# Expert work one scan step later, and the first gate inputs copied inside SBUF, in a fused mixture-of-experts and GRU kernel

## The chip, the cores and the metric

The kernel runs on one core of a Trainium2 chip. Its time is the device time of one execution in microseconds (us), the median of several runs. A profile of one further execution shows every instruction of the engines: TensorE (PE, with its weight loads as PEld), VectorE (DVE), ScalarE (ACT), GpSimd (POOL) and SyncE's DMA queue (SP).

## The reference

The input x is 8 sequences of 512 positions with 256 features. Two stages follow each other.

```
# stage 0: mixture of experts, added to x
shared = silu(x @ w1) * (x @ w3) @ w2
s      = sigmoid(concat(x, cond) @ router_W)         # 8 experts, the best 2 of s + bias
routed = sum_e combine[e] * (gelu(x @ W1e[e]) @ W2e[e])
x = x + (shared + routed) / 3
# stage 1: a GRU over the 512 positions, added to x; H starts as cond
Z = sigmoid(x_t @ Wxz.T + bxz + H @ Whz.T + bhz)
R = sigmoid(x_t @ Wxr.T + bxr + H @ Whr.T + bhr)
C = tanh(x_t @ Wxh.T + bxh + (R * H) @ Whh.T + bhh)
H = Z * H + (1 - Z) * C
out_t = x_t + H @ Whq.T + bhq
```

Everything is float32. The scan has 512 dependent steps. The expert work of a position must be done before its scan step, but it depends on no H.

## The kernel before

**Tiles and pairs.** A tile is 16 positions of the 8 sequences, 128 rows; there are 32 tiles (NT) of 16 scan steps (TS). Expert work goes by pairs of tiles (NPAIR is 16). For a pair it is 144 "up" products (12 units of 12: 4 units of the shared expert, then 8 experts), each 128 x 128 weights by 256 columns, with the operands split into a high and a low part; then for each tile 9 groups of "down" products; then a transpose of the finished tile (x1T), four "projection" products that give the 768 gate inputs in two pieces q of 384 columns with two parts k each (`project`), and, after the tile's scan, two output products of 256 columns (`output`).

**One scan step.** TensorE makes the r product (r_bank, L1247) and the z product (zc_bank) from H (hist). ScalarE makes t_r and t_z, VectorE transposes t_r (t_rT) and makes rhT, TensorE makes the c product (zc_bank<-whT,rhT), ScalarE t_h, VectorE the new H (terms, then a scan instruction into hist). ScalarE also copies ("seeds") the next step's gate inputs into r_bank and zc_bank, from xs.

**Where the expert work stands.** The scan's engines run one written-out order. Each step has a place r from 0 to 31 in a span of two tiles, and a pair number p. `place_of` gives both from the tile n and step s; FIRST_STEP (L274) shifts the whole expert schedule against the scan. `fill_up` puts work between the z and the c product, `fill_rest` behind the c product. Tables say what stands in which place:

- UP_GAP2: five up products in most places, behind the c product; UP_FIRST for pair 1, with five or six in a place. Up products of pair 1 with numbers under FIRST_UPS (36) and the down products of places under FIRST_R run ahead of the scan.
- DOWNS1: down products between z and c. A place takes three halves of 128 columns.
- PROJ1 (L279): the four projection products of a tile, in places 2 to 5 and 18 to 21, between z and c. OUT2: the two output products in place 2 or 18, behind c.
- BIAS2: VectorE's `add_bias` for a finished piece of gate inputs, at the end of a step; FINISH2: `finish_out`, which adds the output product and x; LATE_XT2: the transposes of later input tiles.
- UP_ACT2_FIRST, SILU1_FIRST and HIDDEN1_FIRST: where ScalarE and VectorE take pair 1's finished up products (`consume_up`, `shared_silu`, `shared_hidden`); an up product of a later unit waits for them, since there are two buffers.

**The gate inputs' way.** `add_bias` writes xproj in SBUF. SyncE's queue stores it to DRAM (`store_inputs`, L474), one DMA for each piece, and when the store has landed reads it back into xs (`gate_rows`, L480) with another layout, row = sequence, column = step: four DMAs, one for each of four column groups j, for steps 0 to 7 (semaphore xs_first) and four for steps 8 to 15 (xs_second). For the first tile this stands ahead of the scan. ScalarE waits for xs_first before its first seed. The queue issues in program order and a wait in it holds everything behind it; the loads of later tiles (L464) and the stores of the output stand in the same queue.

## Time and profile before

| what | value |
|---|---|
| median of 3 runs | 1277.98 us (1277.16 to 1278.83) |
| the profiled execution | 1277.44 us, span 1275.5 us |
| PE busy | 1249.8 us, 98% of the span |
| DVE busy | 997.2 us, 78% |
| ACT busy | 803.3 us, 63% |
| DMA | 51.34 MB, mean 40 GB/s |

The span is from the first to the last instruction; the profiled execution's own time has 1.94 us more around it. The ends of matmuls are modelled, so a high busy share of PE is not a proof that TensorE sets the time. The idle time of an engine counts where it stands on the path that ends last.

### The profile page before, as it was taken

Reading aid. Unit: us, or ns where it says so; the run is one execution under the profiler, and the core shown is the slowest. Engines: PE = TensorE matmul, PEld = TensorE weight load, DVE = VectorE, ACT = ScalarE, POOL = GpSimd, SP = SyncE. Lnnn points to the kernel's source line nnn. Section 1 sums busy time; section 2 is a strip of 40 time slices with the busy share of each in tenths; the row PEclk is TensorE's granted clock in tenths of the full one; section 3 lists DMA queues with packets and bytes.
Section 4 is the critical chain, followed back from the end, with each engine's and each line's share of the span. In section 5 each row is a group of like instructions: output and inputs, shape, how many; then the busy total and the mean of one; then the engine's idle time right before and its main releaser. Section 6 shows DMA issues by size and latency. Waiting matters only on the chain.

```text
span 1275.5 us, 84499 instructions
## 1 busy us (share of the span) xinstructions
PE 1249.8 (98%) x35704; PEld 890.8 (70%) x35704; DVE 997.2 (78%) x6111; ACT 803.3 (63%) x4402; POOL 7.4 (1%) x25
## 2 busy tenths in 40 slices
PE   9999999999999999999999999999999999999887
PEld 8877677766677776667776667776667776666554
DVE  6678888788787888878888787887877787877765
ACT  4366666666666666666666666666666666666554
POOL 1000000000000000000000000000000000000000
PEclk9999999999999999999999999999999999999999
DMA  8211011111101111011111101111011111001110
GB/s 273 57 36 43 24 38 30 42 41 34 36 24 39 38 37 45 24 37 27 44 39 35 38 21 41 35 39 45 27 33 27 44 39 33 23 21 27 33 32 11
DMA packets 76186, 51.34 MB, mean 40 GB/s; under 512 B 40609, under 2 KB 73761, under 8 KB 75809
## 3 DMA queue, kind: packets, MB, share of 16 engines
q1 hardware_dynamic: 75128, 45.29, 13.7%
q8 instruction: 281, 4.60, 1.5%
q14 instruction: 97, 0.79, 0.2%
q10 hardware_dynamic: 680, 0.66, 0.2%
HBM read 29.13 MB, written 16.78 MB: 36 GB/s over the span
## 4 chain that ended last, share of the span: by engine, by line
PE 93%; DVE 3%; ACT 2%; issue 1%; DMA 1%; SPq 0%
PE dn_ps L1083 27%; PE up_ps L1111 26%; PE zc_bank L1247 21%; PE r_bank L1247 14%; PE aux L1083 2%; DVE terms L1006 2%; PE dn_ps L1119 1%; ACT t_h L713 1%; PE misc L1083 1%; DVE hist L1009 1%; DMA x_all<-in_L_cond_W1e 1%; DVE t_rT L982 1%; ACT t_r L693 0%; DVE rhT L985 0%; SPq L411 0%
## 5 line engine op out<-in xcount | busy, mean ns | idle before, releaser
L982 DVE STREAM_TRANSPOSE t_rT<-t_r 128x32 f32<-128x32 f32 x1024 | 156.2, 191 | 171.1 <-ACT t_r L693 163.6
L693 ACT ACTIVATE t_r<-r_bank 128x32 f32<-128x32 f32 x1024 | 146.1, 195 | 210.2 <-PE r_bank L1247 200.2
L713 ACT ACTIVATE t_h<-zc_bank 128x32 f32<-128x32 f32 x1024 | 145.9, 195 | 207.7 <-PE zc_bank L1247 207.7
L1083 PE MATMUL dn_ps<-we_sb,x_all 128*32 128x256 f32 (+1 forms) x5144 | 274.5, 329 | 0.0
L1247 PEld LDWEIGHTS zc_bank<-whT,rhT 128*8 128x8 f32 x8192 | 118.1, 87 | 177.5 <-DVE rhT L985 176.9
L1247 PE MATMUL r_bank<-whT,hist 128*8 128x64 f32 x8192 | 210.1, 220 | 16.0 <-DVE hist L1009 13.4
L1247 PE MATMUL zc_bank<-whT,rhT 128*8 128x64 f32 x8192 | 211.0, 220 | 2.8 <-DVE rhT L985 0.3
L1247 PE MATMUL zc_bank<-whT,hist 128*8 128x64 f32 x8192 | 208.9, 219 | 0.8 <-issue 0.8
L1006 DVE STREAM_TRANSPOSE terms<-t_h 128x32 f32<-128x32 f32 x1024 | 156.5, 192 | 38.2 <-ACT t_h L713 19.7
L1247 PEld LDWEIGHTS r_bank<-whT,hist 128*8 128x8 f32 x8192 | 117.6, 88 | 94.6 <-DVE hist L1009 72.5
L1083 PEld LDWEIGHTS dn_ps<-we_sb,x_all 128*32 128x32 f32 x5144 | 137.9, 110 | 31.9 <-issue 1.0
L1111 PE MATMUL up_ps<-x_high,we_high 128*128 128x256 f32 (+1 forms) x540 | 159.1, 295 | 0.2 <-DVE hid L820 0.2
L1111 PE MATMUL up_ps<-x_high,we_low 128*128 128x256 f32 (+1 forms) x540 | 155.4, 288 | 0.0
L1111 PE MATMUL up_ps<-x_low,we_high 128*128 128x256 f32 x526 | 154.9, 294 | 0.0
L624 ACT ACTIVATE zc_bank<-gru_raw 128x128 f32<-128x128 f32 x512 | 144.3, 282 | 16.0
L1009 DVE TENSOR_TENSOR_SCAN hist<-factors,terms 128x16 f32<-128x16 f32 x1024 | 145.4, 184 | 0.0
L1247 PEld LDWEIGHTS zc_bank<-whT,hist 128*8 128x8 f32 x8192 | 142.4, 90 | 0.2
L990 DVE STREAM_TRANSPOSE factors<-a_row 128x64 f32<-128x64 f32 x512 | 126.0, 246 | 19.5 <-ACT a_row L704 1.4
L985 DVE SCALAR_TENSOR_TENSOR rhT<-t_rT,hist 128x8 f32<-128x8 f32 x1024 | 133.3, 168 | 0.0
L704 ACT ACTIVATE a_row<-t_z 128x64 f32<-128x64 f32 x512 | 125.7, 245 | 0.0
L852 DVE SCALAR_TENSOR_TENSOR x_all<-dn_ps,gates_all,x_all 128x256 f32<-128x256 f32 x256 | 121.3, 474 | 5.6 <-PE dn_ps L1119 1.9
L616 ACT ACTIVATE r_bank<-gru_raw 128x64 f32<-128x64 f32 x512 | 114.3, 223 | 3.4 <-DMA gru_raw<-gate_inputs_by_group 3.4
(132 smaller groups left out, 1691.4 us busy)
## 6 DMA issues: line engine op xcount, KB each, us to landing
gate_inputs_by_group<-gru_raw SPq DMA_DIRECT2D x64, 192.0 KB, 2.0
gru_raw<-gate_inputs_by_group SPq DMA_DIRECT2D x256, 48.0 KB
xT_all<-in_x SPq DMA_DIRECT2D x448, 8.0 KB
x_all<-in_x SPq DMA_DIRECT2D x31, 128.0 KB
out<-gru_raw SPq DMA_DIRECT2D x31, 128.0 KB
x_all<-in_L_cond_W1e SPq DMA_DIRECT2D x4, 512.0 KB, 7.6
we_sb<-in_L_cond_W2e SPq DMA_DIRECT2D x4, 512.0 KB, 8.6
xT_all<-in_L_cond_w SPq DMA_DIRECT2D x2, 256.0 KB, 5.3
```

What stands on the lines that cost most here:

```text
L624: act.activation(zc_bank[:, 0:2 * GW], xs[:, s, GW:RW], ACT.Copy).then_inc(seeded_zc, 1)
L693: act.activation(t_r[:, i, :], r_ps[:, i * Q:(i + 1) * Q], ACT.Tanh, scale=0.5).then_inc(tr_ready, 1)
L704: act.activation(a_row[:, :, :], t_z[:, :, :], ACT.Copy, bias=0.5, scale=-0.5).then_inc(a_ready, 1)
L713: act.activation(t_h[:, i, :], c_ps[:, i * Q:(i + 1) * Q], ACT.Tanh, scale=-1.0).then_inc(th_ready, 1)
L982: dve.transpose(t_rT[:, i, :], t_r[:, i, :]).then_inc(trT_done, 1)
L985: dve.scalar_tensor_tensor(rhT[:, i, :], t_rT[:, i, 0:B], 1.0, old[:, i, :], ALU.add, ALU.mult)\
L990: dve.transpose(factors[:, :, :, 1].rearrange("p i q -> p (i q)"), a_row[:, :, :].rearrange("p i q -> p (i q)"))\
L1006: dve.transpose(terms[:, i, :, 0], t_h[:, i, :]).then_inc(thT_done, 1)
L1009: dve.tensor_tensor_scan(hist[:, s, i, :, :].rearrange("p b e -> p (b e)"), factors[:, i, 0:B, :].rearrange("p b e -> p (b e)"), terms[:, ...
L1083: done = pe.matmul(ps[Q * j:Q * (j + 1), col:col + cols], lhsT[:, Q * j:Q * (j + 1)], rhs, start=first, stop=last, tile_position=(0, Q * j ...
L1111: done = pe.matmul(up_ps[place % 2][:, half * PAIR + begin * P:half * PAIR + end * P], w, (x_low if low_x else x_high)[:, p % 2, begin:end ...
L1247: done = pe.matmul(ps[Q * j:Q * j + B, :], lhsT[:, k, :], whT[:, gate, k, j * GW:(j + 1) * GW], start=False, stop=(k == NI - 1), tile_posi ...
```

## The change

FIRST_STEP goes from 6 to 7: every place of the expert schedule comes one scan step later, so place 9 (three halves of down products, two of the up products that were ahead of the scan) is now in step 0. Pair 1's tables are laid out anew: FIRST_UPS is 34, place 18 has no up products, places 9, 25 and 29 have six.

The gate inputs of the following tile keep the step in which they are done. The second part of the first piece moves behind the c product of place 2 or 18 (PROJ2), the second piece is done in places 3 and 4 or 19 and 20. To make room, the output product is cut: 128 of its columns (first part) stay in place 2 or 18, the other 128 and the second part go to place 5 or 21, between z and c. `finish_out` goes there too; `add_bias` goes to places 2 and 4, or 18 and 20.

For the first tile, rows 0 to 2 of xs are filled from xproj directly, SBUF to SBUF, by four DMAs a row (`step_rows`, a semaphore for each row); rows 3 to 7 and 8 to 15 go by DRAM as before. ScalarE waits for each row before its seed. On ScalarE, `score_tanh` moves behind t_h and the zc seed.

```
-        FIRST_STEP = 6
+        FIRST_STEP = 7
...
-        PROJ1 = {2: (-2, 0, 0), 3: (-2, 0, 1), 4: (-2, 1, 0), 5: (-2, 1, 1), 18: (-1, 0, 0), 19: (-1, 0, 1), 20: (-1, 1, 0), 21: (-1, 1, 1)}
+        PROJ1 = {2: (-2, 0, 0), 3: (-2, 1, 0), 4: (-2, 1, 1), 18: (-1, 0, 0), 19: (-1, 1, 0), 20: (-1, 1, 1)}
+        PROJ2 = {2: (-2, 0, 1), 18: (-1, 0, 1)}
         OUT2 = {2: -4, 18: -3}
+        OUT1 = {5: -4, 21: -3}
+        OUT2_PARTS, OUT1_PARTS = [(0, 1, 2)], [(0, 0, 1), (1, 0, 2)]
...
-        UP_ACT2_FIRST = {12: 3, 15: 4, 18: 5, 20: 6, 23: 7, 25: 8, 27: 9, 29: 10, 31: 11}
-        SILU1_FIRST = {10: 2, 13: 3}
-        HIDDEN1_FIRST = {11: 2, 14: 3}
+        UP_ACT2_FIRST = {9: 2, 11: 3, 15: 4, 18: 5, 20: 6, 23: 7, 25: 8, 27: 9, 29: 10, 31: 11}
+        SILU1_FIRST = {10: 2, 12: 3}
+        HIDDEN1_FIRST = {11: 2, 13: 3}
...
-        BIAS2 = {3: (0, -2), 5: (1, -2), 19: (0, -1), 21: (1, -1)}
-        FINISH2 = {2: -4, 18: -3}
+        BIAS2 = {2: (0, -2), 4: (1, -2), 18: (0, -1), 20: (1, -1)}
+        FINISH2 = {5: -4, 21: -3}
...
-        LATE_XT2 = {14: 0, 20: 1}
+        LATE_XT2 = {14: 0, 19: 1}
...
-        FIRST_UPS = 36
+        FIRST_UPS = 34
-        for r in [r for r in range(FIRST_R, SPAN - 1) if r not in LAST_DOWN2]:
-            end = begin + (3 if r in X1_2 else 5 if r in LOGITS2 or r in (12, 13, 14, 25, 29) else 6)
+        for r in [r for r in range(FIRST_R, SPAN - 1) if r not in LAST_DOWN2 and r not in PROJ2]:
+            end = begin + (3 if r in X1_2 else 5 if r in LOGITS2 or r in (12, 13, 14) else 6)
...
+            def step_rows(s, q):
+                for j in range(q * NG // PIECES, (q + 1) * NG // PIECES):
+                    sp.dma_start(xs[Q * j:Q * j + B, s, :], xproj[s::TS, j, :]).then_inc(xs_step[s], 16)
+
             sp.wait_ge(xs_zeroed, 1)
             for q in range(PIECES):
+                sp.wait_ge(xp_ready, q + 1)
+                step_rows(0, q)
+                store_inputs(0, q)
+                for s in range(1, AHEAD):
+                    step_rows(s, q)
+            for q in range(PIECES):
                 sp.wait_ge(xp_stored[q], 16)
-                gate_rows(q, 0, xs_first)
-            sp.wait_ge(xs_first, 16 * NG)
+                gate_rows(q, AHEAD, HALF, xs_first)
             for q in range(PIECES):
-                gate_rows(q, 1, xs_second)
+                gate_rows(q, HALF, TS, xs_second)
...
-            act.wait_ge(xs_first, 16 * NG)
+            act.wait_ge(xs_step[0], 16 * NG)
             seed_r(0, 0)
             seed_zc(0, 0)
-            consume_up(1, 2)
...
                     if after:
+                        if n == 0 and 0 < s + 1 < AHEAD:
+                            act.wait_ge(xs_step[s + 1], 16 * NG)
+                        if n == 0 and s + 1 == AHEAD:
+                            act.wait_ge(xs_first, 16 * NG)
...
-                done = product(aux, 0, C, yst[:, i, :], wqT[:, i, :], i == 0, i == NI - 1)
-                if i == NI - 1:
+                done = product(aux, begin * P, (end - begin) * P, yst[:, i, :], wqT[:, i, begin * P:end * P], opens, i == NI - 1)
+                if (i, begin, end) == OUT1_PARTS[-1]:
                     done.then_inc(y_done, 1)
...
-                    if scan and not downs:
+                    outs = r in OUT1 and 0 <= 2 * p + OUT1[r] < NT - 1
+                    if outs:
+                        for part in OUT1_PARTS:
+                            output(2 * p + OUT1[r], *part)
+                    if scan and not downs and not outs and not (r in OUT1 and 2 * p + OUT1[r] < 0):
                         keep_busy()
...
+                if r in PROJ2 and 0 <= 2 * p + PROJ2[r][0] < NT:
+                    tile, q, k = PROJ2[r]
+                    project(2 * p + tile, q, k)
```

## Rows read from the trace of the kernel before

**Rows 1.** The page's first part: engine, busy us, share of the span, instructions.

```profile
PE 1249.8 (98%) x35704; PEld 890.8 (70%) x35704; DVE 997.2 (78%) x6111; ACT 803.3 (63%) x4402; POOL 7.4 (1%) x25
```

**Rows 2.** Waits: who waited for whom, us in total, times, longest us.

```profile
ACT t_h L713 <- PE zc_bank L1247: 207.7, 481, 0.8
ACT t_r L693 <- PE r_bank L1247: 200.2, 379, 0.8
PEld zc_bank L1247 <- DVE rhT L985: 176.9, 509, 0.6
```

**Rows 3.** The tile t_r, whole span, then from 1113 us: count, ns, first and last start.

```profile
L693 ACT ACTIVATE t_r<-r_bank x1024: 192/195/198, 51.3 to 1269.0; 128x32 f32<-128x32 f32 x171
...
L693 ACT ACTIVATE t_r<-r_bank x132: 192/195/198, 1114.4 to 1269.0; 128x32 f32<-128x32 f32 x132
```

**Rows 4.** Timeline of PE, end of the head and step 0: start us, length us.

```profile
46.69 2.79 PE L1119 MATMUL dn_ps<-we_sb,x_all 128*128 128x256 f32 x16
49.12 0.47 PE L1111 MATMUL up_ps<-x_high,w_high 128*128 128x256 f32 x1
...
49.55 0.28 PE L1111 MATMUL up_ps<-x_high,w_low 128*128 128x256 f32 x1
...
50.61 0.28 PE L1111 MATMUL up_ps<-x_high,w_low 128*128 128x256 f32 x1
50.81 0.41 PE L1247 MATMUL r_bank<-whT,hist 128*8 128x64 f32 x16
...
51.26 0.83 PE L1083 MATMUL dn_ps<-we_sb,x_all 128*32 128x256 f32 x16
...
53.23 0.29 PE L1247 MATMUL r_bank<-whT,hist 128*8 128x64 f32 x6
```

**Rows 5.** Timeline of ACT: the first two seeds, and the next step's r seed.

```profile
50.23 0.23 ACT L616 ACTIVATE r_bank<-gru_raw 128x64 f32<-128x64 f32 x1 [3.40 <-DMA gru_raw<-gate_inputs_by_group]
50.39 0.26 ACT L624 ACTIVATE zc_bank<-gru_raw 128x128 f32<-128x128 f32 x1
...
51.63 0.22 ACT L616 ACTIVATE r_bank<-gru_raw 128x64 f32<-128x64 f32 x1
```

**Rows 6.** Timeline of SP's DMA issues in five stretches.

```profile
23.40 2.43 SPq L452 DMA_DIRECT2D h_rows<-in_cond  x4
...
43.70 1.67 SPq L474 DMA_DIRECT2D gate_inputs_by_group<-gru_raw  x2
45.79 1.80 SPq L480 DMA_DIRECT2D gru_raw<-gate_inputs_by_group  x4
...
86.62 1.30 SPq L480 DMA_DIRECT2D gru_raw<-gate_inputs_by_group  x4
...
1254.76 0.61 SPq L498 DMA_DIRECT2D out<-gru_raw  x1
```

**Rows 7.** Timeline of DVE and PEld in place 11 of pair 1.

```profile
54.64 0.38 DVE L820 TENSOR_TENSOR hid<-gru_raw,up_ps 128x256 f32<-128x256 f32 x1
...
54.97 0.19 PEld L1111 LDWEIGHTS up_ps<-x_high,w_low 128*128 128x128 f32 x1
```

**Rows 8.** Timeline of PE, then DVE, in place 18 of tile 2 and after.

```profile
148.12 1.07 PE L1083 MATMUL aux<-wqT,gru_raw 128*32 128x256 f32 x16
149.01 0.41 PE L1247 MATMUL r_bank<-whT,hist 128*8 128x64 f32 x16
...
149.47 0.83 PE L1083 MATMUL dn_ps<-wxT,x1T 128*32 128x384 f32 x8
...
148.77 0.28 DVE L1009 TENSOR_TENSOR_SCAN hist<-factors,terms 128x16 f32<-128x16 f32 x2
149.25 0.42 DVE L877 TENSOR_TENSOR gru_raw<-aux,x_all 128x256 f32<-128x256 f32 x1 [0.20 <-PE aux L1083]
149.72 0.30 DVE L982 STREAM_TRANSPOSE t_rT<-t_r 128x32 f32<-128x32 f32 x2
```

**Rows 9.** Timeline of DVE: an add_bias in the scan.

```profile
227.43 0.54 DVE L863 TENSOR_TENSOR gru_raw<-dn_ps,bias_rows 128x384 f32<-128x384 f32 x1
```

More of the change, by code:

```diff
@@ L48, in moe_then_gru @@
     HALF = TS // 2
+    AHEAD = 3
     ctx = ExitStack()
@@ L190, in moe_then_gru @@
         xs_second = sem("xs_second")
+        xs_step = [sem(f"xs_step{s}") for s in range(AHEAD)]
         bits_set = sem("bits_set")
@@ L323, in moe_then_gru @@
         for r, tile in OUT2.items():
-            GAP2[r] = in_slots("out", 0, tile, NI)
+            GAP2[r] = [("out", 0, tile, *part) for part in OUT2_PARTS]
         for r, tile in LAST_DOWN2.items():
@@ L474, in store_inputs, with gate_rows @@
                 sp.dma_start(by_group[groups, :, :].rearrange("j p c -> p j c"), xproj[:, groups, :]).then_inc(xp_stored[q], 16)
-            def gate_rows(q, half, done):
+            def gate_rows(q, begin, end, done):
                 for j in range(q * NG // PIECES, (q + 1) * NG // PIECES):
-                    src = by_group[j, :, :].rearrange("(b t) c -> b t c", b=B)[:, half * HALF:(half + 1) * HALF, :]
-                    sp.dma_start(xs[Q * j:Q * j + B, half * HALF:(half + 1) * HALF, :], src).then_inc(done, 16)
-            for q in range(PIECES):
-                store_inputs(0, q)
+                    src = by_group[j, :, :].rearrange("(b t) c -> b t c", b=B)[:, begin:end, :]
+                    sp.dma_start(xs[Q * j:Q * j + B, begin:end, :], src).then_inc(done, 16)
+            def step_rows(s, q):
+                for j in range(q * NG // PIECES, (q + 1) * NG // PIECES):
+                    sp.dma_start(xs[Q * j:Q * j + B, s, :], xproj[s::TS, j, :]).then_inc(xs_step[s], 16)
             sp.wait_ge(xs_zeroed, 1)
             for q in range(PIECES):
+                sp.wait_ge(xp_ready, q + 1)
[4 more added lines that the diff above has]
+            for q in range(PIECES):
                 sp.wait_ge(xp_stored[q], 16)
-                gate_rows(q, 0, xs_first)
-            sp.wait_ge(xs_first, 16 * NG)
+                gate_rows(q, AHEAD, HALF, xs_first)
             for q in range(PIECES):
-                gate_rows(q, 1, xs_second)
+                gate_rows(q, HALF, TS, xs_second)
             load_late(EARLY + 1)
@@ L516, in body @@
                         sp.wait_ge(xp_stored[q], 16 * (n + 2))
-                        gate_rows(q, 0, xs_first)
+                        gate_rows(q, 0, HALF, xs_first)
                 if n % 2 == 0 and 0 < n < NT:
@@ L522, in body @@
                     for q in range(PIECES):
-                        gate_rows(q, 1, xs_second)
+                        gate_rows(q, HALF, TS, xs_second)
                 if n % 2 == 0 and n + EARLY + 2 < NT:
@@ L706, in body @@
                         keep_states(n - 1)
-                    if EARLY <= 2 * p + 2 < NT and r == TANH1:
-                        score_tanh(p, slice(2 * p + 2, 2 * p + 4))
                     if scan:
@@ L719, in body @@
                         consume_up(p, first_or(p, UP_ACT2_FIRST, UP_ACT2)[r])
+                    if EARLY <= 2 * p + 2 < NT and r == TANH1:
+                        score_tanh(p, slice(2 * p + 2, 2 * p + 4))
                     if 0 < p + 1 < NPAIR and r == X_HIGH2:
@@ L1187, in tile_logits, with output @@
                     done.then_inc(logits_done, 1)
-            def output(t, i):
-                if i == 0:
+            def output(t, i, begin, end):
+                opens = (i, begin, end) == OUT2_PARTS[0]
+                if opens:
                     pe.wait_ge(yst_ready, t + 1)
@@ L1237, in fill_rest @@
                     elif kind == "out" and 0 <= t < NT - 1:
-                        output(t, part)
+                        output(t, part, begin, end)
                 if scan and r in UP_GAP2 and not ups:
```

## The prediction

> **What bounds the kernel now.** The page's first part came first: TensorE is busy 98% of the span [rows 1], which would make this a question of TensorE work. The view of waits says otherwise. ScalarE waits 481 times for the c product in zc_bank before t_h and 379 times for r_bank before t_r, while TensorE's weight loads wait 509 times for rhT [rows 2]. Engines that wait for each other in a ring are bound by the ring's latency, and the busy share of PE is filler (expert work) between the gate products. The period of the ring is in t_r, written 1,024 times, twice a step, from 51.3 to 1269.0 us [rows 3]. The second write of a step starts about 0.1 after the first, so the 511 intervals between first writes take 1217.6 us, 2.383 each; in the last 66 steps it is (1268.9 - 1114.4) / 65 = 2.377 [rows 3]. The execution is 50.8 us of head, 512 steps that cost nearly the same whatever filler they hold, and a tail. A change can gain by starting the scan sooner or by shortening steps; moving filler from one step to another gains nothing by itself.
>
> What sets the scan's start is read in two queues. TensorE runs the end of the head without a pause: twelve halves of down products from 46.69, twelve up products from 49.12 to 50.61, and the first gate product at 50.81 [rows 4]. ScalarE's seeds, which need the gate inputs back from DRAM, start at 50.23 and 50.39 and take 0.23 and 0.26 [rows 5]. The r seed is done at 50.46, 0.35 before TensorE asks for it. So a shorter round trip alone would buy nothing, and less TensorE work alone would be stopped by the seed after 0.35 us. Both together move the start.
>
> **The head's TensorE work.** One step of delay takes place 9 out of the head: its three halves of down products and two up products (FIRST_UPS 36 to 34). Twelve halves took 49.12 - 46.69 = 2.43, so three take 0.61. The nine intervals of up products from 49.55 to 50.61 are 0.118 each, so two take 0.24 [rows 4]. The sum is 0.85, and the first gate product could start at 49.96. ScalarE's consume_up that also leaves the head ran behind the seeds, under TensorE's own work, and counts as nothing.
>
> **The seeds.** They now need four SBUF-to-SBUF copies of row 0, and SyncE's queue decides when these go. The first piece's gate inputs are ready at 43.70, where its store was issued [rows 6]. Ahead of the second piece's two row-0 copies the queue now issues two copies (row 0), the store, and four copies (rows 1 and 2). The trace has no such copy. The nearest row is gate_rows, eight destination rows each as here, four issues in 1.30, 0.33 each; the farthest is the load of h_rows, four in 2.43, 0.61 each [rows 6]. With 0.33, and 0.43 for the store, the eight copies are issued by 43.70 + 2.64 + 0.43 = 46.77; the second piece's inputs are there by then, since its old store was issued by 45.37. For the landing, before: the fourth gate_rows issue ended at 45.79 + 1.80 = 47.59 [rows 6] and the seed that waited for it ran at 50.23 [rows 5], 2.64 later. The same here gives 49.41; the other bound, a transfer that takes nothing, gives 46.77. I take 49.41, because even that is early enough: the r seed must start by 49.96 - 0.23 = 49.73, 0.3 of margin. Row 1 (a store of 0.43 and two copies of 0.33 later) lands by 50.50 and is wanted at about 50.8, where step 0's r_bank is seeded for step 1 (0.82 behind the first gate product: 51.63 against 50.81 [rows 4, 5]). If it were late, a_row, t_h and the zc seed would stand behind it on ScalarE, and VectorE and TensorE behind those. Rows 3 to 7 are issued by 50.2, land near 52.8 and are wanted near 55.6. With 0.61 an issue, row 0 is issued by 49.01 and lands at 51.65, and the first gate product moves to 51.9, 1.1 later than before.
>
> **What the first tile pays.** A place with six up products took 50.81 to 53.23, 2.42 [rows 4], 0.04 over 2.377. Pair 1 has ten such places now and twelve after (9, 25 and 29 join, 18 leaves): 0.08. The down products of place 9 go between z and c products, where a group of sixteen matmuls already stands in 0.83 (from 51.26 [rows 4]): no cost. In place 11 the third up product (48) opens unit 4, which waits for shared_hidden of unit 2. In the old place 11 that ran from 54.64 for 0.38, to 55.02, while the third weight load began at 54.97 [rows 7]. With a hand-over of the same size as this gap the stall is 0.1 at most, and nothing if the step's end absorbs it. I take 0.05. Sum: 0.13.
>
> **What every tile pays.** Places 2 and 18 keep 512 columns behind the c product, 384 of the projection and 128 of the output in place of 2 x 256, and places 3 to 5 (19 to 21) keep 384 in front of it. The old place 18 shows that 512 fit: output from 148.12, next r product at 149.01 [rows 8]. What is new there is VectorE's add_bias (0.54 [rows 9]) where finish_out (0.42) stood. finish_out started at 149.25, when all 512 columns were done, and ended at 149.67, 0.05 before the next t_rT. The projection comes first of the 512, so its 384 columns are done 0.2 sooner; add_bias then starts where the scan instruction ends, 148.77 + 0.28 = 149.05, and ends at 149.59 [rows 8]. Slack 0.13: no cost. In places 5 and 21 finish_out's product is done half a step before it. score_tanh stood in ScalarE's wait for the c product [rows 2], which covered it; behind the seed it has the wait for r_bank as cover. Out stores come four steps (9.5 us) later: the last but one moves from 1254.76 [rows 6] to 1264.3, before the last t_r at 1269.0 [rows 3], and finish_last, which waits for it, comes later still. The tail keeps its length.
>
> One rule of the Trainium skill speaks against this part: "TensorE: Matmul & The Clock Gate", section "Wait — 56ns, not 53.3ns?", says that without hardware decode a matmul costs the sequencer about 62 ns, which binds small ones. Eight more of them in place 5 would be 0.5 us, and by that estimate, with nothing hidden, the sum would be -0.72 + 31 x 0.5 = +14.8. The rows disagree: sixteen matmuls of 128 and 256 columns take the same 0.83 as eight of 384 [rows 4, 8].
>
> **Sum.** -0.85 + 0.08 + 0.05 = -0.72 us. The profiled execution took 1277.44 (span 1275.5 and 1.94 around it), so it becomes 1276.7. It is 0.54 under the median of the runs shown, 1277.98, so the median becomes 1277.26; I say 1277.3. About 0.2%, 2.56 us, is what a measurement of this kernel can tell from no change, and the three runs of before are 1.7 apart. The likeliest case's own range is 1276.3 to 1278.2.
>
> **Rivals.**
> 1. Row copies late. For it: eight copies and a store share one queue, and the h_rows row shows issues twice as long. Against it: gate_rows, the nearest shape, does not. At 0.61 an issue: 1277.98 + 1.1 + 0.13 = 1279.2. Chance 0.17.
> 2. The other side: add_bias in places 2 and 18 comes too late and pushes t_rT, once in each of 31 tiles. If it started where finish_out did, 149.25, it would end at 149.79, 0.07 over: 31 x 0.07 = 2.2, so 1279.4. It is slower by 2.56 from (2.56 + 0.72) / 31 = 0.106 a tile, when add_bias starts at 149.29 or later, 0.24 behind my reckoning. Against it: its 384 columns come before the other 128. Chance 0.10, half of it beyond 0.2%.
> 3. Many small matmuls bind by their number. The output's sixteen in 1.07 [rows 8] are 0.067 each; if that is a price per matmul and not per column, place 5 takes 1.07 in place of 0.83: 31 x 0.24 = 7.4, 1284.7. Against it: sixteen in 0.83. Chance 0.02.
> 4. No effect: the start does not move, because something that the seeds' 0.35 of lead hid binds next. 1277.98 + 0.13 = 1278.1. Chance 0.06.
> 5. More than a start: the steps' excess over their floor, 1217.6 - 511 x 2.377 = 3.0 us [rows 3], falls away with the new placement. 1277.26 - 3.0 = 1274.3. Nothing speaks for it but that the excess exists. Chance 0.04.
> My forecast has 0.61.
>
> **Range and chances.** Cases 1 and 2 pull the top to 1279.4. Below, case 5 stays out, and the spread of medians moves the likeliest case's 1276.3 down to 1275.8. Faster by over 0.2%: 0.05, case 5 and the edge of the spread. Slower: 0.05 from case 2, 0.02 from case 3. Within: 0.88.
>
> **What the profile of the changed kernel would show.** Right: the first seed by 49.7 and the first r product near 50.0; the time from the last t_r to the end unchanged; add_bias in places 2 and 18 ended before the next t_rT; the steps from the second tile on at 2.38. Wrong: a first seed after 49.75; ScalarE held for row 1 in step 0; in places 2 and 18 a t_rT that starts only when add_bias ends; or any place that is over 2.38 in every tile.

## The result, and the profile of the kernel after

The changed kernel takes 1280.87 us, the median of 22 runs (1278.82 to 1284.62), and the kernel before, run beside it, 1278.45 (22 runs, 1276.40 to 1281.59). The ratio is 1.0016, with a 95% interval of 1.0008 to 1.0023: slower by about 2.4 us, within 0.2% but clearly not the 0.7 us less that was forecast, and above the range. (The forecast was added to 1277.98, the median of three runs; on the 1278.45 measured here it would have been 1277.7, so 0.5 us of the distance is the starting point.) Two later comparisons, each on a chip of its own, gave +1.25 and +0.08 us (below), so 2.4 is the largest of three. Five executions of the second comparison took 1641 to 2842 us, those of before among them, and are left out of all medians, means and intervals.

The first part of the page of the kernel after, as [rows 1]:

```profile
PE 1250.5 (98%) x35958; PEld 895.9 (70%) x35958; DVE 994.5 (78%) x6111; ACT 803.5 (63%) x4402; POOL 7.4 (1%) x25
```

No engine's busy time has changed by more than 0.6%. In the view of waits the ring is that of [rows 2]. The last row was 0.8 us, once, in the kernel before: weight loads of the cut output stand idle 61 times, 0.2 each, with nothing that the profile sees ahead of them; the places where they stand are no longer for it (below).

```profile
ACT t_h L727 <- PE zc_bank L1271: 211.0, 480, 1.1
ACT t_r L705 <- PE r_bank L1271: 200.1, 385, 1.0
...
PEld zc_bank L1271 <- DVE rhT L1001: 169.9, 505, 0.7
...
PEld aux L1099 <- issue: 12.4, 61, 0.8
```

The tile t_r, over the whole span (count, least, median and longest ns, first and last start), as [rows 3]:

```profile
L705 ACT ACTIVATE t_r<-r_bank x1024: 192/195/198, 51.1 to 1272.7; 128x32 f32<-128x32 f32 x171
```

The scan starts 0.16 sooner (51.13 against 51.29) and its last step is 3.7 us later. So in this pair of profiles the loss lies inside the scan. Where it starts, SyncE's queue and ScalarE's seeds, as [rows 6] and [rows 5]:

```profile
43.82 1.27 SPq L490 DMA_DIRECT2D gru_raw<-gru_raw  x2
45.13 0.44 SPq L479 DMA_DIRECT2D gate_inputs_by_group<-gru_raw  x1
45.62 3.62 SPq L490 DMA_DIRECT2D gru_raw<-gru_raw  x6
49.28 0.44 SPq L479 DMA_DIRECT2D gate_inputs_by_group<-gru_raw  x1
49.77 2.41 SPq L490 DMA_DIRECT2D gru_raw<-gru_raw  x4
```

```profile
50.37 0.23 ACT L629 ACTIVATE r_bank<-gru_raw 128x64 f32<-128x64 f32 x1 [3.41 <-DMA gru_raw<-gru_raw]
...
51.13 0.28 ACT L705 ACTIVATE t_r<-r_bank 128x32 f32<-128x32 f32 x2 [0.33 <-PE r_bank L1271]
51.35 0.23 ACT L707 ACTIVATE t_z<-zc_bank 128x64 f32<-128x64 f32 x1
52.10 0.23 ACT L629 ACTIVATE r_bank<-gru_raw 128x64 f32<-128x64 f32 x1 [0.52 <-DMA gru_raw<-gru_raw]
```

A row copy (L490) takes 0.60 to 0.64 us of SyncE's queue, and the eight copies and the store are issued at 49.24. The r seed runs 1.13 later, at 50.37, still waiting for its data; row 1 holds the next r seed until 52.10. TensorE's timeline, as [rows 4]:

```profile
46.82 2.13 PE L1135 MATMUL dn_ps<-we_sb,x_all 128*128 128x256 f32 x12
...
49.85 0.28 PE L1127 MATMUL up_ps<-x_high,w_high 128*128 128x256 f32 x1
50.65 0.41 PE L1271 MATMUL r_bank<-whT,hist 128*8 128x64 f32 x16 [0.53 <-ACT r_bank L629]
...
53.39 0.41 PE L1271 MATMUL r_bank<-whT,hist 128*8 128x64 f32 x16 [0.25 <-DVE hist L1025]
...
55.81 0.41 PE L1271 MATMUL r_bank<-whT,hist 128*8 128x64 f32 x16
...
58.38 0.30 PE L1271 MATMUL r_bank<-whT,hist 128*8 128x64 f32 x8
```

Its work is shorter as reckoned: the last up product starts at 49.85 in place of 50.61. It then stands idle for the seed until 50.65 (0.53). Step 0 takes 53.39 - 50.65 = 2.74, step 1 2.42, step 2 2.57, where a steady one takes 2.375. Against [rows 4]'s 2.42 for step 0, row 1 costs 0.32. In step 2 (place 11), as in [rows 7], unit 4 waits for shared_hidden:

```profile
57.27 0.38 DVE L836 TENSOR_TENSOR hid<-gru_raw,up_ps 128x256 f32<-128x256 f32 x1
```

```profile
57.71 0.39 PE L1127 MATMUL up_ps<-x_high,we_high 128*128 128x256 f32 x1
```

In the middle of the scan, place 18 of tile 2, as [rows 8] (TensorE, then VectorE):

```profile
150.59 0.83 PE L1099 MATMUL dn_ps<-wxT,x1T 128*32 128x384 f32 x8
151.24 0.40 PE L1099 MATMUL aux<-wqT,gru_raw 128*32 128x128 f32 x8
...
156.77 0.83 PE L1099 MATMUL aux<-wqT,gru_raw 128*32 128x128 f32 x16
```

```profile
151.52 0.53 DVE L879 TENSOR_TENSOR gru_raw<-dn_ps,bias_rows 128x384 f32<-128x384 f32 x1
152.28 0.30 DVE L998 STREAM_TRANSPOSE t_rT<-t_r 128x32 f32<-128x32 f32 x2 [0.22 <-ACT t_r L705]
```

add_bias ends at 152.05 and the next t_rT waits for ScalarE, not for it; the sixteen small output matmuls of place 21 take 0.83. At each of the 32 places the median step of this profile is 2.373 to 2.377, so no place is longer in every tile. What remains are single long steps, whose length is worked out from the starts of t_r. The largest is step 305, 3.49 us, on TensorE:

```profile
779.94 0.39 PE L1271 MATMUL zc_bank<-whT,hist 128*8 128x64 f32 x11
781.19 0.29 PE L1271 MATMUL zc_bank<-whT,hist 128*8 128x64 f32 x5 [0.87 <-issue]
```

Sixteen products of one group are torn after the eleventh, and TensorE stands idle for 0.87 us. "issue" says only that it waited for nothing that the profile shows; that its next instruction was missing is an inference, taken up below. The kernel before has the same kind of stop (0.78 at 969.19). Summed over the 511 intervals, what the steps take beyond 2.376 each ("the excess") is 3.45 in the profile of before and 7.31 in that of after; 0.31 and 0.73 of it lie in the first tile. (The expectations below call the two 2.9 and 7.8, which are the same sums over floors of 2.377 and 2.375.)

### The profile page after: what moved, and what is told of

Read it like the earlier page. It is cut to its first block, busy times and chain, and to the rows that moved or that the text cites. A ratio compares the mean times of both kernels' runs of the same rounds, so it can differ in the third digit from the quotient of the medians.

```text
span 1279.2 us, 85022 instructions
## 1 busy us (share of the span) xinstructions
PE 1250.5 (98%) x35958; PEld 895.9 (70%) x35958; DVE 994.5 (78%) x6111; ACT 803.5 (63%) x4402; POOL 7.4 (1%) x25
## 4 chain that ended last, share of the span: by engine, by line
PE 91%; DVE 4%; ACT 2%; issue 1%; SPq 1%; DMA 1%; DVEq 0%
PE dn_ps L1099 27%; PE up_ps L1127 25%; PE zc_bank L1271 21%; PE r_bank L1271 14%; PE aux L1099 2%; DVE terms L1022 2%; ACT t_h L727 1%; PE dn_ps L1135 1%; PE misc L1099 1%; DVE hist L1025 1%; DMA x_all<-in_L_cond_W1e 1%; ACT t_r L705 1%; DVE t_rT L998 0%; SPq L490 0%; DVE rhT L1001 0%
```

## The experiments

Each was run on one chip beside the kernel before. "Difference" is the mean of its runs minus the mean of those of before, with a 95% interval worked out from the spread of both. "First t_r" and "excess" are those of the one profiled execution.

| run | median, before beside it | ratio, 95% | difference | first t_r | excess |
|---|---|---|---|---|---|
| e1 rows by DRAM | 1279.07, 1279.38 | 0.9999, 0.9991 to 1.0008 | -0.1 ± 0.9 | 50.99 | 4.78 |
| e3 split only | 1278.22, 1279.38 | 0.9996, 0.9986 to 1.0006 | -0.6 ± 1.1 | 51.56 | 6.24 |
| e4 rows only | 1279.44, 1279.38 | 1.0001, 0.9991 to 1.0011 | +0.4 ± 1.0 | 51.82 | 5.95 |
| e7 full forms | 1314.05, 1279.38 | 1.0270, 1.0257 to 1.0284 | +34.7 ± 0.9 | 50.86 | 40.6 |
| e5 changed again | 1281.60, 1279.80 | 1.0009, 0.9996 to 1.0021 | +1.3 ± 1.4 | 50.92 | 6.22 |
| e6 rows by DRAM again | 1280.37, 1279.80 | 1.0000, 0.9990 to 1.0011 | 0.0 ± 1.1 | 51.58 | 5.58 |
| e8 two queues | 1278.75, 1279.80 | 0.9991, 0.9980 to 1.0001 | -1.4 ± 1.1 | 50.56 | 3.97 |
| e9 uncut output | 1288.78, 1279.80 | 1.0071, 1.0053 to 1.0089 | +9.1 ± 2.1 | 51.00 | 19.1 |
| e10 stream moved 32 | 1283.32, 1280.57 | 1.0032, 1.0016 to 1.0049 | +3.8 ± 1.9 | 53.13 | 7.53 |
| e11 stream moved 80 | 1280.18, 1280.57 | 0.9995, 0.9986 to 1.0004 | -0.5 ± 0.8 | 51.45 | 6.82 |
| e12 no block loads | 1280.65, 1280.57 | 1.0005, 0.9996 to 1.0015 | +0.3 ± 1.1 | 51.16 | 5.52 |
| e13 two queues again | 1281.33, 1280.57 | 1.0003, 0.9992 to 1.0014 | +0.3 ± 1.3 | 51.23 | 4.51 |
| f1 changed, third | 1279.33, 1279.08 | 1.0003, 0.9992 to 1.0014 | +0.1 ± 1.1 | 50.84 | 4.28 |
| f2 rows by DRAM, third | 1279.82, 1279.08 | 1.0011, 0.9997 to 1.0024 | +1.3 ± 1.4 | 50.97 | 10.34 |
| f3 two queues, third | 1280.28, 1279.08 | 1.0003, 0.9989 to 1.0017 | +0.5 ± 1.3 | 52.99 | 4.01 |
| f4 vector stream moved | 1282.31, 1279.08 | 1.0025, 1.0012 to 1.0039 | +3.0 ± 1.4 | 53.14 | 4.87 |

The first t_r moves with the whole head from one execution to the next: SyncE's first issue for the gate inputs, which marks when their first piece is ready, is at 43.70 in before and at 43.48 to 46.36 elsewhere. Counted from that issue, the first t_r hardly scatters:

| kernel | profiles | issue to first t_r |
|---|---|---|
| before, e3, e4 (old step) | 3 | 7.59, 7.64, 7.61 |
| new step with the row copies of the change | 9 | 7.31 or 7.32 |
| new step, rows by DRAM (e1, e6, f2) | 3 | 7.43, 7.43, 7.49 |
| new step, two queues (e8, e13, f3) | 3 | 6.72, 6.71, 6.64 |

So the change brings 0.28 of the start that was forecast to come 0.85 sooner, rows by DRAM 0.10 to 0.16, and two queues 0.87 to 0.95.

**The parts, one at a time.** e1 keeps the new expert order and the cut output, and brings all eight rows by DRAM:

```diff
             for q in range(PIECES):
-                sp.wait_ge(xp_ready, q + 1)
-                step_rows(0, q)
                 store_inputs(0, q)
-                for s in range(1, AHEAD):
-                    step_rows(s, q)
...
-                gate_rows(q, AHEAD, HALF, xs_first)
+                gate_rows(q, 0, HALF, xs_first)
```

> The changed kernel with the first tile's rows taken by DRAM again, as before; the shift and the cut output product stay. Theory A (TensorE runs out of instructions more often, since the cut output product adds sixteen of them a tile): the scan's excess over 511 x 2.376 us stays near the 7.8 us of the changed kernel's profile, against 2.9 before, and the time stays 2 us or more over before. Theory B (the late row copies and the stall of step 2 are the loss): the 0.36 us of step 0 goes, the seed comes at about 50.4 as it did with the copies, and the time falls back to within 0.3 us of before.

e3 has the moved output and projection products alone, at the old step (`FIRST_STEP = 6`, `FIRST_UPS = 37`, `PROJ2`, `OUT1`, the new due times, no step_rows):

> The kernel before with the cut output product and the new places of projection and bias only: FIRST_STEP 6, rows by DRAM, 37 up products ahead of the scan. Theory A (more instructions a tile): excess of 5 us or more in the scan, time 2 us over before. Theory C (the shift against the late loads makes the stalls, not the cut): excess near 3 us and the time within 0.5 us of before. Theory B also says within 0.5.

e4 is the kernel before with step_rows and its waits alone:

> The kernel before with the row copies of the change only. Theory B: the first seed near 50.4, the first r product near 50.8 as before, step 0 longer by 0.3 to 0.4 us because row 1 lands late, time 0.3 to 0.4 over before. Theories A and C say the same of this one: no more stalls for instructions than before, excess 3 to 3.5 us.

None of the three can be told from before by its time, so theory A's 2 us over before is missed by e1 and e3; but e3 has the excess of over 5 that A names (6.24), and e4's 5.95 is outside what all theories said for it. Their first tiles can be told. In e1 step 0 is as long as it was (2.42), as theory B says, and the excess of the first tile is 0.36; the first t_r comes 0.16 sooner by the table of starts. The shorter TensorE work pays a little without any row copy. In e4 the seed runs at 50.76, 6.55 after the first piece of gate inputs is ready (SyncE issues its first copy at 44.21); in before that time was 50.23 - 43.70 = 6.53 [rows 5, 6]. And row 1 holds step 0:

```profile
50.76 0.23 ACT L626 ACTIVATE r_bank<-gru_raw 128x64 f32<-128x64 f32 x1 [3.41 <-DMA gru_raw<-gru_raw]
...
52.49 0.23 ACT L626 ACTIVATE r_bank<-gru_raw 128x64 f32<-128x64 f32 x1 [0.23 <-DMA gru_raw<-gru_raw]
```

So twelve copies in one queue make the seed no sooner than the round trip through DRAM did, and step 0 takes 2.62.

**The cut output.** e9 is the changed kernel with the output product whole and the four projection places where they were, add_bias and finish_out with them, and the up products laid out to fit:

```diff
-        PROJ1 = {2: (-2, 0, 0), 3: (-2, 1, 0), 4: (-2, 1, 1), 18: (-1, 0, 0), 19: (-1, 1, 0), 20: (-1, 1, 1)}
-        PROJ2 = {2: (-2, 0, 1), 18: (-1, 0, 1)}
+        PROJ1 = {2: (-2, 0, 0), 3: (-2, 0, 1), 4: (-2, 1, 0), 5: (-2, 1, 1), 18: (-1, 0, 0), 19: (-1, 0, 1), 20: (-1, 1, 0), 21: (-1, 1, 1)}
+        PROJ2 = {}
...
-        OUT1 = {5: -4, 21: -3}
-        OUT2_PARTS, OUT1_PARTS = [(0, 1, 2)], [(0, 0, 1), (1, 0, 2)]
+        OUT1 = {}
+        OUT2_PARTS, OUT1_PARTS = [(0, 0, 2), (1, 0, 2)], [(1, 0, 2)]
...
```

> The changed kernel (one step later, row copies) with the projection, bias and output places of before, uncut: the gate inputs of the next tile are done one step later. If the cut is what keeps them in time, as the change says, ScalarE waits for DMA at the end of each tile, before the r seed: bias add in step 12 ends near 31 us after a tile's start, store 2.0, four reads 1.3, landing 2.6, together 37, against the 37.4 at which the seed is due: a wait of 0 to 1 us a tile, 0 to 30 us in all. Theory A, had it stood, says 2 us less than the changed kernel.

It is 9.1 us slower than before, 7.9 ± 2.5 slower than the changed kernel beside it (e5). Thirteen of the tiles end in a step 0.3 to 1.8 too long, like this one (step 63, ScalarE, the seed of the next tile):

```profile
201.84 0.22 ACT L707 ACTIVATE t_z<-zc_bank 128x64 f32<-128x64 f32 x1
203.56 0.23 ACT L629 ACTIVATE r_bank<-gru_raw 128x64 f32<-128x64 f32 x1 [1.50 <-DMA gru_raw<-gate_inputs_by_group]
```

In e9 SyncE starts the store of these gate inputs at 192.20, 9.4 ahead of that step's first t_r (201.62); in the changed kernel at 190.99, 11.9 ahead of it (202.90). That step is what the cut buys: it gains nothing, it keeps the delay of the expert work from costing some 8 us.

**Row copies in two queues.** e8 puts row 0 of both pieces at the front of SyncE's queue, then both stores, then row 2; it issues row 1 from ScalarE's queue, and places 9 and 12 trade one up product, so that the first product of unit 4 is the fourth of place 11 and not the third:

```diff
                 step_rows(0, q)
+            for q in range(PIECES):
                 store_inputs(0, q)
-                for s in range(1, AHEAD):
-                    step_rows(s, q)
+            for q in range(PIECES):
+                step_rows(2, q)
...
+            act.wait_ge(xs_zeroed, 1)
+            act.wait_ge(xp_ready, PIECES)
+            for j in range(NG):
+                act.dma_start(xs[Q * j:Q * j + B, 1, :], xproj[1::TS, j, :]).then_inc(xs_step[1], 16)
             act.wait_ge(xs_step[0], 16 * NG)
```

> A version that mends what the trace of the changed kernel shows in the first tile: row 0 of both pieces goes first on SyncE's queue, row 1 is issued from ScalarE's queue, which is idle there, then the stores, then row 2; places 9 and 12 of pair 1 trade one up product, so that up product 48 is the fourth of place 11. By the issue time of 0.61 us and the landing 1.13 us after the last issue's end: seed at 47.8 at the earliest, after ScalarE's own issues at 49.4, first r product at 50.0, step 0 at 2.38 to 2.42, step 2 at 2.42. 1.0 us less than the changed kernel by theory B, 0.6 to 0.9 less than before; the stops for instructions may hide it.

```profile
43.85 2.49 SPq L490 DMA_DIRECT2D gru_raw<-gru_raw  x4
...
47.37 3.00 SPq L490 DMA_DIRECT2D gru_raw<-gru_raw  x4
```

```profile
46.67 2.53 ACTq L696 DMA_DIRECT2D gru_raw<-gru_raw  x4
49.31 0.23 ACT L630 ACTIVATE r_bank<-gru_raw 128x64 f32<-128x64 f32 x1 [2.31 <-issue]
...
50.56 0.28 ACT L710 ACTIVATE t_r<-r_bank 128x32 f32<-128x32 f32 x2 [0.83 <-PE r_bank L1276]
...
50.96 0.22 ACT L630 ACTIVATE r_bank<-gru_raw 128x64 f32<-128x64 f32 x1
```

Row 0 is issued by 46.34, and the seed (49.31) waits for no data, only for ScalarE's own four issues, which end at 49.20. TensorE's own work sets the start at last (50.56, 0.73 before that of before), and row 1's seed follows in its place. Step 0 is 2.38 and step 2 is 2.45. This is the gain that the prediction had reckoned, and the comparison gave -1.4. How much of it the order of the copies brings and how much the second queue was not separated. Again, twice:

> The mended version again, for its ratio: 0.9991 before, 0.998 to 1.0001. By the first tile alone it should be 0.4 to 0.9 us under the kernel before, so 0.9993 to 0.9997, and 1.2 us under the changed kernel.

> The changed kernel with the row copies in SyncE's and ScalarE's queues, the scan starting some 0.7 us sooner. Its two comparisons so far gave -1.4 and +0.3 us against before. Theory A: 0.7 us under the form without row copies or more, so -1 to 0 us against before. Theory B: 0 to +1. If it lies above before, the sooner start isn't kept over the scan.

They gave +0.3 and +0.5. In both profiles the head itself was late (first t_r at 51.23 and 52.99), while the time from the first piece to the first t_r was again 6.6 to 6.7. Over the three comparisons the mean, each weighted by its interval, is -0.3 ± 0.7. That interval holds 0 and also the -0.8 to -1.0 to which start and first tile come in the three profiles: the sooner start is seen in every profile, and the times neither confirm nor refute it.

**The changed kernel and its form without row copies, repeated.**

> The changed kernel again, beside e6 and the kernel before on one chip. Theory D (the difference is made of stops for instructions that fall differently in each execution and each load of a program; the change itself costs 0.1 to 0.4 us): the ratio to before comes back nearer to 1 than 1.0016, within 1.0005, and the excess of its profile is not 7.8 us again. Theory E (the changed kernel's own instruction streams make more stops): 1.0016 again, excess of 6 us or more.

> The changed kernel with rows by DRAM, again. TensorE's and VectorE's instruction order is that of the changed kernel. Theory D: within 0.4 us of e5 and within 0.5 of before. Theory F (the row copies cost 1.5 us or more together with the shift, in some way that I do not see in the first tile): e5 over e6 by 1.5 us or more, e6 equal to before.

> The changed kernel itself, beside the next three. Theory A (the row copies cost 0.45 us in the first tile and the rest of the difference is the chance of where TensorE's instruction stream is cut): 0.4 to 2 us over the kernel before, and over the form without row copies by the same. Theory B (every kernel with the new order of expert work has more stops): as much over before, and the form without row copies as well. Theory C (the excess seen in the first comparison was mostly the chip it ran on): within 0.5 us of before.

> The new expert order and cut output, with all eight rows of the first tile through DRAM as before. Theory A: within 0.5 us of before, 0.4 to 2 us under the changed kernel. Theory B: 1 to 2 us over before. Theory C: within 0.5 us of both.

Beside each other, the changed kernel lies 1.2 above the form by DRAM in one comparison and 1.2 below it in the next, ± 1.6 and ± 1.5. Of the theories before e5, D's ratio (within 1.0005) was missed with 1.0009, though its interval holds it, and its other part came (the excess fell); E's excess of 6 came (6.22) and its 1.0016 didn't; F's 1.5 us isn't reached. None of the three put before f1 and f2 is borne out by both; nearest is that both forms are the same. Three differences of the changed kernel from before (+2.46 ± 0.9, +1.25 ± 1.4, +0.08 ± 1.1) weigh up to +1.4 ± 0.6, but the first and the third don't agree with one another within their intervals. What all three profiles of it share is the start (7.31 behind the first piece) and the first tile: the row-1 wait is 0.52 each time (seeds at 51.89 and 51.81 in e5 and f1), step 0 is 0.36 too long, and step 2 0.19.

f2 shows what else moves a run. It is the kernel of e1, and its profiled execution took 1284.58 against 1279.03. The excess of its steps is 10.34 against 4.78, 5.6 more, and that is all the difference. Its largest stop is at step 144:

```profile
397.16 0.39 PE L1264 MATMUL r_bank<-whT,hist 128*8 128x64 f32 x10
398.80 0.24 PE L1264 MATMUL r_bank<-whT,hist 128*8 128x64 f32 x3 [1.25 <-issue]
```

**Where the stops come from.** If they lay where a fetched block of TensorE's instructions ends, moving the stream would move them; e10 and e11 put 8 and 20 more matmuls into the warm-up (32 and 80 instructions):

```diff
-            warm(8)
+            for _ in range(16):
+                pe.matmul(aux[:, 0:P // 2], zeros[:, :], zeros[:, 0:P // 2], start=True, stop=True).then_inc(warmed, 1)
```

> The changed kernel with the eight warm-up products of TensorE's start as sixteen of half the width: 32 more instructions at the very start, the same columns, everything after them in the same order. Steps that are long in every execution of the changed kernel (numbered from the scan's start: 47, 56, 103, 134, 153, 182, 260, 308, 337) must be caused by where TensorE's stream of instructions is cut for fetching, or by the work in them. Theory G (by the cuts): those steps are at 2.38 now and others are long. Theory H (by the work): the same steps are long.

> The same with 80 more instructions ahead (24 products of 8 columns and four warm-up products in place of eight). Theory G: a third set of long steps. The head may differ by a few tenths. Time within 1 us of the changed kernel by both, or up to 1 us lower if the cuts of the changed kernel are unlucky ones.

e10's warm-up took 7.1 us in place of 3.8 (its first t_r is at 53.13), so its time says nothing on stops. Of the nine steps that were named, 47, 56, 103 and 337 are at 2.40 or less in both, as theory G has it; but 47 and 103 come and go between e1, e6 and f2 as well, which are one kernel, and 56 (2.72, 2.45, 2.40) between the three profiles of the changed kernel. The large stops came elsewhere in both. They aren't spread at random, though: step 161 (3.01) and step 305 (3.48 or 3.49) are long by the same amount in the first profile of the changed kernel, in e6 and in f2, and at 2.38 or less in e5 and f1.

The other five small ones (steps 134, 153, 182, 260 and 308, mostly 0.09 to 0.17 over) stand at the same steps in every kernel above with the new order, in e10 and e11 too. They don't hang on TensorE's stream. f4 moves VectorE's:

```diff
             dve.memset(zeros[:, :], 0.0).then_inc(zeros_ready, 1)
+            for _ in range(20):
+                link(dve.memset(rden[:, :], 0.0))
```

> The changed kernel with twenty memsets on VectorE in its idle time before 6.5 us of the head, each with its wait; nothing of the scan changes. Theory V (the long steps 134, 153, 182, 260 and 308, +0.10 to +0.17 us each in every kernel with this order, are VectorE waiting for its own instructions): they move to other steps. Rival (they come from a coincidence of work in the tile or of a transfer): they stay at the same steps. The time stays within 0.5 us of the changed kernel either way.

None of the five is long in f4. Step 134 on VectorE, changed kernel, then f4:

```profile
372.26 0.30 DVE L998 STREAM_TRANSPOSE t_rT<-t_r 128x32 f32<-128x32 f32 x2 [0.33 <-ACT t_r L705]
...
373.15 0.18 DVE L1017 SCALAR_TENSOR_TENSOR terms<-factors,hist 128x16 f32<-128x16 f32 x1
373.54 0.31 DVE L1022 STREAM_TRANSPOSE terms<-t_h 128x32 f32<-128x32 f32 x2 [0.21 <-ACT t_h L727]
...
374.74 0.30 DVE L998 STREAM_TRANSPOSE t_rT<-t_r 128x32 f32<-128x32 f32 x2 [0.29 <-ACT t_r L705]
```

```profile
374.02 0.30 DVE L1000 STREAM_TRANSPOSE t_rT<-t_r 128x32 f32<-128x32 f32 x2 [0.33 <-ACT t_r L705]
...
374.90 0.18 DVE L1019 SCALAR_TENSOR_TENSOR terms<-factors,hist 128x16 f32<-128x16 f32 x1
375.19 0.31 DVE L1024 STREAM_TRANSPOSE terms<-t_h 128x32 f32<-128x32 f32 x2
...
376.39 0.31 DVE L1000 STREAM_TRANSPOSE t_rT<-t_r 128x32 f32<-128x32 f32 x2 [0.29 <-ACT t_r L705]
```

From the terms product to the transpose behind it passes 0.39 in the one and 0.29 in the other, and the step from t_rT to t_rT takes 2.48 and 2.37. So these five hang on where VectorE's stream stands, and the name of the releaser in the row (t_h) is only the last one that the profile knows. A late start is no rival: e10's scan starts as late as f4's, and its five steps are long. That the engine waited for its instructions there is inferred, since the row doesn't say "issue", but the transfers of instructions, which the trace has too (queue q14, 8 KB each), speak for it: in the three profiles of the changed kernel, in e10 and in e11 one of them starts 2.1 to 2.9 us into each of the five steps, about 1 us behind VectorE's gap, and in f4 it comes some 4 us sooner. The expectation on f4's time missed: it is 3.0 us over before, and its profile shows why for one execution (the head, below).

TensorE's instructions come in 16 KB transfers by queue q8. The page of the changed kernel, then that of e7 (below), which has fewer matmuls and ten fewer transfers:

```profile
q8 instruction: 283, 4.64, 1.6%
```

```profile
q8 instruction: 273, 4.47, 1.4%
```

Such a transfer takes 1.1 us as a rule. The one ahead of step 305 (777.9) took 1.86, the one ahead of step 144 in f2 (395.1) 2.30, the one ahead of the 0.78 us stop of before (965.9) 1.86. Over all profiles but e7 and e9, 14 of the 27 transfers of 1.7 us or more are followed within some 4 us by a step more than 0.3 us too long, and 35 of the 4,093 under 1.4 us. Of the 26 steps that are more than 0.6 us too long, 14 have one of 1.5 us or more ahead of them. So about half of the large stops go with a slow transfer of TensorE's instructions. That is a coincidence in time, found in traces and not brought about by an edit; the other half has no such mark, and what makes a transfer slow is open.

Last, whether the stops come of the block loads that move at the same time: in e12 tiles 6 to 31 take their transposed input from the blocks of tiles 4 and 5, so its output differs.

```diff
-                for j in range(NG):
+                for j in range(NG if t < EARLY + 2 else 0):
```

> The changed kernel without the sixteen small loads of the transposed input blocks for tiles 6 to 31; later tiles are computed from the blocks of tiles 4 and 5, so the values of the output are others. 416 DMAs of 64 short rows each go. If the long stops of TensorE for instructions (0.3 to 1.1 us) come from fetches that wait behind this traffic, the excess of the scan falls from 5 to 8 us to 2 us or less, and the time by 2 to 4 us. If they come from the fetches themselves, it stays.

Its excess is 5.52, inside the 4.28 to 7.31 of the changed kernel's three profiles and far from the 2 that was named, and its time is that of before (+0.3 ± 1.1). So the loads aren't what makes most of the stops. The five small ones are absent here too, and e12 has one more wait on VectorE in each such tile, which moves VectorE's stream as f4 does.

**Matmuls of another width.** e7 gives the output and projection products their 128-column weights whole (full_product) in place of four of 32:

```diff
-                done = product(aux, begin * P, (end - begin) * P, yst[:, i, :], wqT[:, i, begin * P:end * P], opens, i == NI - 1)
+                done = full_product(aux[:, begin * P:], (end - begin) * P, yst[:, i, :], wqT[:, i, begin * P:end * P], opens, i == NI - 1)
```

> The changed kernel with its projection and output products as single 128-wide matmuls in place of four of 32 columns of the array: 84 fewer TensorE instructions a tile than the changed kernel, the same columns streamed. Theory A (fewer instructions, fewer stops for them): excess falls under that of the kernel before, to 2 us or less, and the time goes below before by 0 to 1 us. Theories B and C: excess stays near 7 us and the time 2 us over before.

It is 34.7 us slower: four steps of every tile, those of places 2 to 5 and 18 to 21, are 0.23 to 0.43 longer. The products of step 25, place 2:

```profile
112.86 0.91 PE L1135 MATMUL dn_ps<-wxT,x1T 128*128 128x384 f32 x2
113.70 0.41 PE L1271 MATMUL zc_bank<-whT,rhT 128*8 128x64 f32 x16
114.04 0.91 PE L1135 MATMUL dn_ps<-wxT,x1T 128*128 128x384 f32 x2
```

From two full ones to what follows them it is 0.84 (112.86 to 113.70) between the z and c products and 0.75 (114.04 to 114.79) behind; with eight cut ones of the same work it is 0.73 (149.64 to 150.37 in the changed kernel) and 0.65 (150.59 to 151.24). The number of matmuls was not the price; fewer of them were dearer. Theory A's 2 us or less and B's and C's 7 us of excess were all missed.

## Why the prediction was wrong

The likeliest case and its mechanism (both limits of the start move together) didn't come, and two of the prediction's own signs of being wrong did: a first seed after 49.75 (50.37), and ScalarE held for row 1 in step 0. Rival 1, with 0.17, had the price of an issue right and the landing wrong.

- **What bounds the kernel; steps don't care what filler they hold.** Right for this change: the median step is 2.375 to 2.377 in every kernel of this order. Two runs show where it ends: in e9 filler makes the next tile's gate inputs late, in e7 it is too long for its place.
- **The head's TensorE work, -0.85.** Right in size: from the first of the last down products to the last up product it is 3.03 in place of 3.92, 0.89 less. In e8, where nothing else binds, the first t_r is 0.87 sooner behind the first piece of gate inputs.
- **"The seeds" is the step that failed.** It took 0.33 an issue from gate_rows as the nearest shape; a row copy takes 0.60 to 0.64, the other bound (h_rows, 0.61). Eight copies and a store were issued at 49.24, not 46.77. The time to land was wrong the other way: 2.64 was taken, 1.13 was measured from the end of the last issue. The two errors cancel in part, by luck, so the seed ran at 50.37, between the forecast's 49.41 and rival 1's 51.65, and left 0.28 of the 0.85 (0.16 by the clock of this pair of profiles, whose heads differ by 0.12). From gate inputs to seed it took 6.55, the round trip 6.53.
- **Row 1.** The prediction said what would stand behind a late row 1, and dismissed it with the same 0.33. It was 0.52 late to ScalarE and cost 0.36 in step 0 (against the steady step; 0.32 against the old step 0).
- **Place 11.** 0.05 was taken, 0.1 called the most; step 2 was 0.19 over. With the excess of the first tile 0.42 more than in before (0.73 and 0.31; 0.50 more in e5 and f1), start and first tile come to -0.28 + 0.42 = +0.1 (+0.2 in e5 and f1), in place of -0.72.
- **What every tile pays, nothing.** Right, as far as steady steps show: add_bias ends 0.23 before t_rT (0.13 forecast), sixteen output matmuls take 0.83, and rivals 2 and 3 don't occur.
- **The tail.** Right: from the last t_r to the end of the span 6.6 us before and after.
- **The constant around the span.** The sum kept 1.94 us beside the span. It isn't constant: nearly every execution has 1.8 to 2.2 there or 2.4 to 3.2. The mean of the four later sets of before is 2.19 (123 runs; for the first comparison its spans are not on record); of the changed kernel 2.66, 2.65 and 2.60 (44 runs), of e3 and e11 1.86 over all of their runs. So about 0.45 us of the changed kernel's loss lies outside the span. The row copies aren't the reason, since the forms by DRAM (2.63, 2.51, 2.43) have it too, and e11, the changed kernel with another warm-up, doesn't. Why one kernel has more of the long ones was not tried.
- **The steps' excess as constant.** 3.0 was kept (3.45 over 2.376); profiles of kernels that differ little show 4 to 10. This swings a single execution more than the change does.

Of the mean difference of +1.4 ± 0.6 us, 0.45 lies outside the span and 0.1 to 0.2 in the start and the first tile. The rest, about 0.8, is not explained: it is within what the stops' scatter leaves open, and so is whether the first comparison's 2.4 was more than that scatter. What is shown, then, is why the gain did not come (some 0.9 of the 2.1 us between -0.7 and +1.4); the failed step alone would have left the time inside the stated range (1278.45 + 0.1), and why the kernel is slower than before, if it is by more than 0.6, stays open.

## What to carry to other kernels

Price a DMA issue by the queue time of a row with the same source, target and pattern, and where there is none, take the far bound as the forecast when many issues stand in one queue ahead of a consumer: here 0.33 against 0.61 times eight took two thirds of the gain in the start, and the late row 1 the rest. Put the copies that the first consumer waits for at the front of the queue, and those for the second behind them or into another queue (the seed at 49.31 in place of 50.37). Measure a start from an event of its own head, which here takes out up to 2.9 us of scatter. And before forecasting a change under 0.2%, count what one execution's stops are worth: two profiled executions of one kernel differed by 5.6 us by them alone.

## What was not expected of the hardware

In f3 and f4 the scan starts 2 us late, at 52.99 and 53.14. In f3 nothing that was changed is near; f4 has its twenty memsets on VectorE ahead of it, so for f4 the edit can't be ruled out. TensorE's timeline in f3, then its windows (the granted clock is the third number from the right):

```profile
7.90 0.50 PE L1312 MATMUL up_ps<-x_high,w_low 128*128 128x256 f32 x2
10.03 0.51 PE L1312 MATMUL up_ps<-x_high,w_high 128*128 128x256 f32 x2 [1.63 <-ACT w_high L617]
```

```profile
11.00:13.00 2.00, 2.00 (x13) 2.00 (x13) 1.74 (x4) 0.67 (x2) 0.00 (x0) 0.60 0.93 290
13.00:15.00 2.00, 2.00 (x12) 2.00 (x12) 0.95 (x3) 1.39 (x3) 0.00 (x0) 0.54 1.05 332
```

ScalarE's split of a weight waited 2.31 us for its load, TensorE stood idle for 1.63 behind it, and from 11.4 to 14.7 us it had the lower of its two clocks (1.2 GHz), its up products following one another every 0.21 in place of 0.117. Against e8, the same kernel, the thirteenth up product starts 0.98 later (11.09 and 10.11) and the thirty-first, behind the slow stretch, 2.53 later (15.20 and 12.67). So the idle time costs 1.0 and the clock 1.5, and together they make the start of 52.99 out of 50.56. In e13, the same kernel again, TensorE stood idle for 0.97 at this point and the granted clock stayed at 1.00. A load that lands late in the first 10 us thus costs more than this change could have brought; f4 shows the same wait (TensorE idle for 1.43) and a granted clock of 0.82 from 9 to 12 us and 0.62 from 12 to 15.
